# A selective-scan kernel on one core: du made by VectorE, the product by C of slot 8 by GpSimd

## The reference

```python
def step(h, inp):
    u_t, d_t, b_t, c_t = inp
    dA = jnp.exp(d_t[:, :, None] * A)
    h = dA * h + (d_t * u_t)[:, :, None] * b_t[:, None, :]
    y = jnp.einsum('bdn,bn->bd', h, c_t)
```

## Time and profile before

| | |
|---|---|
| median of three runs | 2149.23 us |
| profiled execution | 2150.92 us |
| its span, first to last instruction | 2149.1 us |
| busy share of the span: VectorE, TensorE, ScalarE, GpSimd | 90%, 87%, 78%, 68% |
| L845 (once per step) in two neighbouring steps | starts at 868.84 and 920.03 us |
| last scan (L814) | starts at 1711.0 us; behind it the experts' part to the end |

### The profile page before, as it was taken

How to read it: one execution, slowest core, us unless ns; L and a number is a source line. 1 busy time by engine, 2 the same in 40 slices (tenths; PEclk the granted TensorE clock), 3 DMA queues, 4 the chain that set the end, 5 groups by cost and what they waited for, 6 DMA issues and landing times.

```text
span 2149.1 us, 34575 instructions
## 1 busy us (share of the span) xinstructions
PE 1868.8 (87%) x10784; PEld 1177.3 (55%) x10784; DVE 1940.8 (90%) x1822; ACT 1683.6 (78%) x3053; POOL 1457.5 (68%) x1364
## 2 busy tenths in 40 slices
PE   4688888888888888888888888888888699999998
PEld 2344444444444444444444445444444499998998
DVE  3699999999999999999999999999999987767775
ACT  3799989999899999999999999999999433333333
POOL 2588888888888888888888888888889600000000
PEclk8899999999999999999999999999999999999999
DMA  8333332323232323232323333332322200000000
GB/s 246 75 78 76 77 76 64 78 62 78 62 78 62 78 62 79 65 81 65 81 73 74 81 77 84 74 82 62 78 62 72 84 1 11 11 11 10 10 6 11
DMA packets 73289, 139.45 MB, mean 65 GB/s; under 512 B 13072, under 2 KB 31120, under 8 KB 68624
## 3 DMA queue, kind: packets, MB, share of 16 engines
q1 hardware_dynamic: 66832, 120.32, 23.1%
q10 hardware_dynamic: 6400, 18.42, 3.7%
HBM read 63.85 MB, written 7.74 MB: 33 GB/s over the span
## 4 chain that ended last, share of the span: by engine, by line
POOL 26%; ACT 26%; PE 23%; issue 12%; DVE 3%; ACTq 1%; POOLq 0%; DVEq 0%
POOL scan L469 13%; POOL scan L463 12%; ACT decay L548 11%; PE y_ps L1253 11%; PE dbu_ps L1228 8%; ACT scan L626 6%; DVE scan L814 2%; POOL scan L460 2%; ACT sp_e L585 1%; ACT delta L586 1%; ACT sp_l L595 1%; ACT sp_e L590 1%; PE dbu_ps L1048 1%; ACT du_t L611 1%; PE y_ps L1033 1%
## 5 line engine op out<-in xcount | busy, mean ns | idle before, releaser
L814 DVE TENSOR_TENSOR_SCAN scan<-decay,dbu_ps 128x1024 f32<-128x1024 f32 x512 | 1155.0, 2274 | 41.6 <-PE dbu_ps L1048 36.1
L1048 PE MATMUL dbu_ps<-ident,scan 128*128 128x128 f32 x4096 | 572.0, 286 | 237.4 <-DVE scan L814 200.9
L469 POOL TENSOR_TENSOR scan<-scan,c_rep 128x1024 f32<-128x1024 f32 x255 | 671.9, 2635 | 143.6 <-DVE scan L814 79.0
L1048 PEld LDWEIGHTS dbu_ps<-ident,scan 128*128 128x128 f32 x4096 | 480.2, 146 | 517.8 <-DVE scan L814 266.5
L548 ACT ACTIVATE decay<-d_rep,a_cur 128x510 f32<-128x510 f32 x1024 | 668.0, 709 | 65.0 <-DMA d_rep<-delta 23.6
L463 POOL TENSOR_SCALAR scan<-du_t,b_t 128x256 f32<-128x256 f32 x896 | 594.0, 678 | 0.0
L626 ACT ACTIVATE scan<-du_t,b_t 128x256 f32<-128x256 f32 x1024 | 445.6, 494 | 1.2
L823 DVE TENSOR_TENSOR scan<-scan,c_rep 128x1024 f32<-128x1024 f32 x257 | 332.6, 1294 | 0.0
L751 ACT ACTIVATE decay<-dbu_ps 128x512 f32<-128x512 f32 x256 | 148.1, 597 | 206.1 <-PE dbu_ps L1228 184.1
L1033 PE MATMUL y_ps<-scan,sel 128*32 128x512 f32 x2048 | 298.4, 658 | 0.0
L1061 PE MATMUL pre_ps<-xn,w_pre 128*128 128x512 f32 x512 | 249.8, 611 | 5.5 <-DVE w_pre L803 4.7
(11 more groups left out here) (107 smaller groups left out, 1625.5 us busy)
## 6 DMA issues: line engine op xcount, KB each, us to landing
d_rep<-delta SPq DMA_DIRECT2D x512, 128.0 KB, 2.9
c_rep<-c_rows SPq DMA_DIRECT2D x32, 1024.0 KB
w_pre<-prepared_weights ACTq DMA_DIRECT2D x15, 866.0 KB, 12.6
prepared_weights<-scan SPq DMA_DIRECT2D x3, 1122.0 KB, 13.3
scan<-in_conv_w SPq DMA_DIRECT2D x4, 512.0 KB, 4.8
w_out<-prepared_weights SPq DMA_DIRECT2D x16, 128.0 KB, 12.3
sp_e<-in_x_rows SPq DMA_DIRECT2D x8, 256.0 KB, 3.3
d_rep<-in_w ACTq DMA_DIRECT2D x2, 1024.0 KB, 7.6
```

The lines of the kernel that those rows point to most:

```text
L469: nc.gpsimd.tensor_tensor(ring[slot % RING], ring[slot % RING], c_rep[par][:, slot // PRS, :].unsqueeze(1).broadcast_to([128, 2, TG]), ALU ...
L814: nc.vector.tensor_tensor_scan(ring[slot % RING].rearrange("p u t -> p (u t)"), decay[slot % DEC].rearrange("p u a t -> p (u a t)"), dbu_p ...
L1048: last = nc.tensor.transpose(dbu_ps[slot % 2][:, u, 128 * j:128 * j + 128], dbu_t[m % 2][:, j, b, :, :].rearrange("p q c -> p (q c)"), ide ...
```

## The change

GpSimd no longer makes du; VectorE makes it right behind delta, between scan 8 and scan 9, after a wait for its own delta. The product by C of slot 8 goes from VectorE (where it stood behind scan 9) to GpSimd, which has it in its slot 9, behind the two outer products there. VectorE has seven products per step, GpSimd nine, and the waits count accordingly.

```diff
--- before.py
+++ after.py
@@ -37,6 +37,8 @@
 
 
 
+C_POOL = [c for c in range(M * PRS) if c % 2 or c == M * PRS // 2]
+C_DVE = [c for c in range(M * PRS) if c not in C_POOL]
 LOG_SCALE = 3.0 ** -0.5
 LOG_BIAS = -0.75 * LOG_SCALE
 LOG_ADD = 13.0 / 16.0
@@ -390,8 +392,8 @@
                     replicate(s + 1, nxt)
                 if is_last(s):
                     sp.wait_ge(skip_done, STEPS)
-                    sp.wait_ge(hc_dve, SLOTS // 2 * (STEPS - 1))
-                    sp.wait_ge(hc_pool, SLOTS // 2 * (STEPS - 1))
+                    sp.wait_ge(hc_dve, len(C_DVE) * (STEPS - 1))
+                    sp.wait_ge(hc_pool, len(C_POOL) * (STEPS - 1))
                     for e in range(EXPERTS):
                         sp.dma_start(w2_sb[e], w2[e, :, :].rearrange("(c p) d -> p c d", p=128))\
                             .then_inc(w2_loaded[e // half], 16)
@@ -474,17 +476,13 @@
                 nxt = 1 - par
                 for slot in range(SLOTS):
                     m = slot // PRS + 1
-                    if slot == 10 and has(s, 1):
-                        pool.wait_ge(delta_ready, s + 2)
-                        nc.gpsimd.tensor_tensor(du[:, :, :], delta[:, :, :], xc[nxt][:, :, :], ALU.mult)\
-                            .then_inc(du_ready, 1)
                     if m < M and has(s, 0):
                         outer(s, par, m, POOL_SHARE[slot % PRS], POOL_SHARE[slot % PRS + 1])
                     if m == M and has(s, 1):
                         outer(s + 1, nxt, 0, POOL_FIRST[slot % PRS], POOL_FIRST[slot % PRS + 1])
                     if slot == 0 and has(s, -1) and has(s, 0):
                         times_c(s - 1, i if par else i - 1, nxt, SLOTS - 1)
-                    elif slot % 2 == 0 and slot and has(s, 0):
+                    elif slot - 1 in C_POOL and has(s, 0):
                         times_c(s, i, par, slot - 1)
                     if slot == 7 and has(s, 2):
                         normalise(s + 2)
@@ -572,8 +570,8 @@
                 nc.scalar.activation(dbc[:, :], pre_ps[0][0:NBC, :], ACT.Copy).then_inc(dbc_ready, 1)
                 act.wait_ge(dbc_ready, s + 1)
 
-                wait(act, hc_dve, SLOTS // 2 * (s - 1))
-                wait(act, hc_pool, SLOTS // 2 * (s - 1))
+                wait(act, hc_dve, len(C_DVE) * (s - 1))
+                wait(act, hc_pool, len(C_POOL) * (s - 1))
                 act.dma_start(c_dram[par, :, :], dbc[RANK + NS:NBC, :]).then_inc(c_stored, 16)
 
             def softplus_parts(s):
@@ -832,7 +830,7 @@
                 for slot in range(SLOTS):
                     if has(s, 0):
                         scan(s, slot)
-                        if slot % 2:
+                        if slot - 1 in C_DVE:
                             times_c(s, i, par, slot - 1)
                     if has(s, -1):
                         if slot == 2:
@@ -852,6 +850,9 @@
                             dve.wait_ge(dve_sp, 2 * (s + 1) + 2)
                             nc.vector.tensor_tensor(delta[:, :, :], delta[:, :, :], sp_l[:, :, :], ALU.add)\
                                 .then_inc(delta_ready, 1)
+                            dve.wait_ge(delta_ready, s + 2)
+                            nc.vector.tensor_tensor(du[:, :, :], delta[:, :, :], xc[1 - par][:, :, :], ALU.mult)\
+                                .then_inc(du_ready, 1)
                     if is_last(s):
                         if slot == 6:
                             residual(0, 0)
@@ -1026,8 +1027,9 @@
             def quad(s, m, k):
 
                 extra = 1 if is_last(s) and m == M - 1 and k == KT - 1 else 0
-                pe.wait_ge(hc_dve, SLOTS // 2 * s + 2 * m + k + 1 + extra)
-                pe.wait_ge(hc_pool, SLOTS // 2 * s + 2 * m + k + 1 - extra)
+                end = PRS * m + 2 * k + 2
+                pe.wait_ge(hc_dve, len(C_DVE) * s + sum(c < end for c in C_DVE) + extra)
+                pe.wait_ge(hc_pool, len(C_POOL) * s + sum(c < end for c in C_POOL) - extra)
                 for j in range(Q):
                     slot = PRS * m + 2 * k + j // 2
                     last = nc.tensor.matmul(y_ps[k][CH * j:CH * j + CH, :], sel[:, :],
```

## The result

The changed kernel took 2246.91 us in the median of four runs (2241.33 to 2250.09), against 2149.89 of the kernel before in its four: a ratio of 1.044 (95% interval 1.0419 to 1.046), 97 us more. The profiled execution has a span of 2246.8 us. It is slower, by 22 us more than the forecast of 2225 us, and inside the range (2190 to 2256).

A forecast was written before the change was run, and what follows sets the result against it. It took the once-per-step ring of hand-overs over du_t as the bound: 31 x 2.5 = 77.5 us more, less 1.1 for the first du, on 2150.9 us gives 2227, less 1.7 for the median: 2225 us, range 2190 to 2256.

The forecast's parts named there:

- GpSimd's product goes ahead of delta: Between L849 and L853 on VectorE: waiting product 8 takes the turn, so scan 9 starts 3.53 us later.
- The upper price: VectorE's chain waits for a whole GpSimd product (2.35 us), not the 0.16 us of the steady rows.
- The ring: Once per step: ScalarE's du_t copies, GpSimd's products, TensorE's transposes, ScalarE's queue; grows 2.0 to 2.75 us, 2.5 taken.
- the lateness of the copies: ScalarE's copies of du_t come later: 2.3 us in the mean with fast clock, 3.05 with slow.
- 0.3 for product 11: On GpSimd: product 11, held by VectorE's product 10 in every second step, now starts behind it, saving 0.3 us.
- I go a little over halfway: TensorE's idle gap grows from 4.55 to 8.1 us; copies' lateness taken between fast and slow clock cases.
- the slow case: TensorE's clock stays at 0.50 through du's transposes (1.97 instead of 1.09 us); copies 3.05 us late in the mean.
- Rival 1: Slow clock through du's transposes every step and product 11 still meets a VectorE product: 3.35 us per step, 2252 us, chance 0.12.
- VectorE's spare 0.72 us: Idle time before L845 that could take up part of VectorE's 2.2 us growth per step, leaving at least 1.5.
- Rivals 2 and 3: VectorE keeps its turn: 2159 us, chance 0.10; the same with fast clock when du is turned: 2142 us, chance 0.06.
- rival 3: VectorE keeps its turn and TensorE's clock is fast when du is turned: -0.22 us per step, 2142 us, chance 0.06.
- the lower end of the forecast's range: 2209 us, from the low end of the ring's growth, 2.0 us per step; range 2209 to 2234, chance 0.72.

The follow-up runs named there:

- Experiment 2: Changed kernel with GpSimd waiting for VectorE's du before product 8: 2163.27 us; changed kernel with product 8 behind product 9, no such wait: 2181.61 us.
- each part alone: Against the kernel before: only du moved to VectorE, 2189.14 us; only product 8 moved to GpSimd's slot 9, 2194.88 us.
- the added wait: Changed kernel, but GpSimd waits for VectorE's du before it begins product 8: 2163.27 us, 1.0054 to the kernel before.
- the kernel with product 11 first: Kernel before, but GpSimd waits for the copies of du_t behind product 11 instead of ahead of it: 2149.41 us, 0.9991.

## Why the prediction was right, and what was mis-sized

- **GpSimd's product goes ahead of delta: right, nearly to the number.** The forecast had product 8 ending at x+4.88, L853 at x+5.99, scan 9 at x+7.36; the trace has x+4.87, x+5.96 and x+7.30. Experiment 2 shows that about 85 of the 97 us hang on what GpSimd puts into the chain, 67 of them on this product. The upper price, taken from one row of another stage, was the true one.
- **The ring: right.** In all fourteen kernels (before, after and the twelve of the experiments) the mean time from a step's first transposes (slot 0 on TensorE) to the next step's chain is 28.8 to 29.0 us, while the time from the chain to these transposes is 22.5 us before, 25.7 after, 24.5 with the gap filled, 24.0 and 23.8 with each part alone, 22.9 with the added wait. All of the difference between them lies in the second stretch, where the copies of du_t stand. In the eleven kernels that keep the order of the outer products behind product 11, a step also grows by what the end of product 11 moves from x: by 3.34 us for 3.24 in the changed kernel, and to within 0.15 us in each.
- **The term that was too small: the lateness of the copies.** It was put at 2.3 us with the fast clock, 3.05 with the slow one, and a mixture was taken, less 0.3 for product 11: 2.5. The trace has the copies' end 3.45 us late in the mean (x+15.98 for x+12.53), less 0.2 for product 11: 3.3. "I go a little over halfway" failed: the clock was slow through du's transposes in every steady step. And the working of the slow case counted only the first copy's start; the second waited for du's second half, so the pair took 1.37 us and not 1.06. The forecast's mixture left out 0.25 us by the clock, 0.14 by a first copy still later than its slow case, and 0.26 by the pair. By the steady steps the sum is 31 x 3.3 = 102 us, less 1.1; 97 were measured, since the first four steps grew by 9 us instead of 13. Rival 1, 2252 us, had the clock right and product 11 wrong, which never met VectorE's product: it came nearer than the forecast with one of its two conditions right.
- **VectorE's spare 0.72 us was none.** The prediction let VectorE's path take up a part of its idle time before L845. This wait has 0.6 to 0.7 us in the mean in all kernels, for the chain's first instruction waits for ScalarE on the same ring. It did not change the forecast, since the ring was taken.
- **Not foreseen: VectorE waits for slot 12's transposes** (39.3 us in 28 steps), since they too run slow. The ring accounts for the growth of a step without it; no run separates it.
- **Rivals 2 and 3** (VectorE keeps its turn) are out: in every steady step the waiting product went between the second and the third instruction.
- **Small slips.** By its own terms rival 3 comes to 2141 us and the lower end of the forecast's range to 2210, a microsecond from the 2142 and 2209 named. Nothing hangs on them.

## What to carry to other kernels

Before work goes to an engine that has idle time, look at what the receiving engine will meet at that place: here a product of 2.35 us was put beside a chain of dependent two-input instructions of VectorE, and the chain paid for it at once. Where an engine stands in a wait, that wait may be what protects the chain; about 85 us came back by adding one. And follow the ring of hand-overs rather than the busy shares: moving two short instructions ahead of a long one on the ring gave 0.7%, while a product per step taken from the busiest engine gave nothing, for that engine then waited in its next product as long as the work had taken.

## What the runs showed of the hardware

- GpSimd's products and outer products, and VectorE's instructions with two inputs in SBUF, exclude each other for whole instructions, in both directions: 3.26 us for 1.23 on VectorE, 3.31 for 2.36 on GpSimd. The one that was held ends 0.14 to 0.15 us less than its own duration behind the other. Between two dependent VectorE instructions of the chain the GpSimd instruction that has waited goes first: product 8 in all steady steps, and outer products of 0.47 us too, which cost the chain 0.15 us a turn.
- The Trainium skill has the first of these (SBUF — State Buffer, "SBUF: two separate sides": whichever "starts first gets the pair for the whole instruction"), and the traces here agree, with the 2.03 us more on L851 beside a product of 2.36.
- Behind an idle gap of TensorE of 8.0 us the clock was at its lower level for 10.2 us of every steady step, behind one of 4.55 us for 5.5 in the mean; but with the same gap of 4.55 us it was 3.4 in every steady step of the kernel with product 11 first, so the length of the gap doesn't give it alone. With the gap filled by repeated transposes it was none, worth some 37 us in the changed kernel and nothing in the kernel before.
